# TensorE's fillers before the second loop over slots cut from 26 to 3, and two of four tile sums moved from TensorE to VectorE and GpSimd

## What is computed

```python
x = x + 0.5 * ffn(layernorm(x))
x = x + attn(layernorm(x))          # gated linear attention in chunks of 64
x = x + 0.5 * ffn(layernorm(x))

def ffn(x):                          # 16 experts of width 176, 4 for each token
    shared = silu_and_mul(x @ shared_gate_up_w.T) @ shared_down_w.T
    shared = shared * sigmoid(x @ sgate_w.T)
    topk_w, topk_ids = top_k(softmax(x @ gate_w.T), 4)
    ...
        coef = sum(where(topk_ids == e, topk_w, 0))
        acc = acc + (silu_and_mul(x @ w13_e.T) @ w2_e.T) * coef
    return shared + acc
```

## Time and profile before

| | us |
|---|---|
| median of 3 runs | 464.55 (464.35 to 465.01) |
| the profiled execution, its own time | 462.54 |
| its span, first to last instruction | 460.7 |
| TensorE busy | 422.1 (92% of the span) |
| VectorE busy | 279.0 (61%) |
| ScalarE busy | 215.2 (47%) |
| GpSimd busy | 197.3 (43%) |

### The profile page before, as it was taken

How to read it: one execution, slowest core, us unless ns; L and a number is a source line. 1 busy time by engine, 2 the same in 40 slices (tenths; PEclk the granted TensorE clock), 3 DMA queues, 4 the chain that set the end, 5 groups by cost and what they waited for, 6 DMA issues and landing times.

```text
span 460.7 us, 9122 instructions
## 1 busy us (share of the span) xinstructions
PE 422.1 (92%) x2288; PEld 327.5 (71%) x2293; DVE 279.0 (61%) x871; ACT 215.2 (47%) x575; POOL 197.3 (43%) x213
## 2 busy tenths in 40 slices
PE   6698985999999999996997988999999999999997
PEld 3455552888887999562477975655679999999855
DVE  5646968566565666297287546634256666666554
ACT  2265636455555666251755642211036666656510
POOL 6177840144444444490044413777114444444530
PEclk9599998899999999997998989999999999999999
DMA  7999942456667442740000008994314444444174
GB/s 253 379 407 233 357 161 58 159 194 218 248 247 293 145 138 79 296 200 0 0 0 1 2 1 338 421 364 153 102 50 128 143 133 138 140 131 134 71 298 168
DMA packets 37376, 80.41 MB, mean 175 GB/s; under 512 B 5680, under 2 KB 27056, under 8 KB 35824
## 3 DMA queue, kind: packets, MB, share of 16 engines
q1 hardware_dynamic: 29744, 58.07, 37.4%
q0 software_dynamic: 7584, 21.77, 12.7%
HBM read 44.28 MB, written 35.54 MB: 173 GB/s over the span
## 4 chain that ended last, share of the span: by engine, by line
PE 77%; DVE 11%; issue 3%; POOL 3%; ACT 3%; DMA 2%; DVEq 0%; SPq 0%
PE ps L466 7%; PE ps L517 7%; PE ps L521 7%; PE ps L518 7%; PE ps L488 6%; PE ps L500 6%; PE ps L471 5%; PE ps L529 4%; PE ps L642 4%; PE ps L547 3%; POOL WR L1029 3%; PE ps L549 2%; PE ps L548 2%; PE ps L553 2%; PE ps L551 2%
## 5 line engine op out<-in xcount | busy, mean ns | idle before, releaser
L986 POOL DMA_INDIRECT results<-ar,idx x94 | 90.4, 962 | 146.7 <-ACT ar L815 143.5
L978 POOL DMA_INDIRECT slots<-XR,pos x64 | 65.3, 1021 | 45.6 <-DVE pos L1159 27.0
L1199 DVE SCALAR_TENSOR_TENSOR ar<-ps,XR,ar 128x176 f32<-128x176 f32 x94 | 37.7, 401 | 66.8 <-ACT ar L801 66.8
L517 PE MATMUL ps<-WH,xt 128*128 x188 | 63.1, 336 | 5.7 <-issue 4.1
L518 PE MATMUL ps<-WL,xt 128*128 x188 | 61.2, 326 | 0.0
L801 ACT ACTIVATE ar<-ps 128x176 f32<-128x176 f32 x94 | 29.9, 318 | 64.9 <-PE ps L521 64.1
L488 PE MATMUL ps<-WS,ar 128*128 128x256 f32 (+1 forms) x192 | 45.7, 382 | 4.0 <-DVE ar L1079 2.3
L488 PEld LDWEIGHTS ps<-WS,ar 128*128 128x128 f32 (+1 forms) x192 | 35.8, 189 | 18.2 <-issue 7.9
L521 PE MATMUL ps<-WH,xl 128*128 x188 | 46.8, 331 | 1.2 <-DVE xl L1216 1.2
L1216 DVE TENSOR_TENSOR xl<-ps,xt 128x256 fp32r<-128x256 f32 x94 | 39.9, 424 | 12.3 <-ACT xt L796 5.6
L466 PE MATMUL ps<-XT,WS 128*128 128x512 f32 x96 | 47.2, 616 | 0.0
(11 more groups left out here) (164 smaller groups left out, 844.1 us busy)
## 6 DMA issues: line engine op xcount, KB each, us to landing
XR<-slots SPq DMA_DIRECT2D x94, 144.0 KB, 2.2
WR<-results SPq DMA_DIRECT2D x16, 512.0 KB, 6.9
WR<-w SPq DMA_DIRECT2D x4, 1408.0 KB, 15.6
wl<-WL SPq DMA_DIRECT2D x4, 1408.0 KB, 5.6
WL<-wl SPq DMA_DIRECT2D x4, 1408.0 KB, 10.1
slots<-zeros SPq DMA_DIRECT2D x33, 144.0 KB
W2R<-w2a SPq DMA_DIRECT2D x1, 2048.0 KB, 23.8
w2l<-W2L SPq DMA_DIRECT2D x1, 2048.0 KB, 7.1
```

Of the source, the lines that this page charges most:

```text
L517: pe.matmul(to, token, WH[:, bass.ds(e, 1), k, :].rearrange("p a n -> p (a n)"), start=k == 0, stop=False)
L978: pool.indirect_dma_start(out=slots_dram[:, :], out_offset=bass.IndirectOffsetOnAxis(ap=pos[:, t, r:r + 1], axis=0), in_=XR[:, t, :], in_o ...
L986: pool.indirect_dma_start(out=results_dram[:, :], out_offset=bass.IndirectOffsetOnAxis(ap=idx[:, i:i + 1], axis=0), in_=ys[i % NY], in_off ...
```

## The change

There are three edits. The 18 fillers in front of the second loop's first transposes are gone, and the 8 behind them are 3. The border between the two ways of summing is moved from `NT // 2` = 4 to `SUMMED` = 6: tiles 4 and 5 of the second feed-forward stage go the way of tiles 0 to 3. The semaphore counts in `added_to` and `combine` follow.

```diff
+        SUMMED = NT - 2
+
         def by_tensor(f, t):
-            return f == 1 and t >= NT // 2
+            return f == 1 and t >= SUMMED
...
-            return 2 * NT + 3 * min(t + 1, NT // 2) + max(t + 1 - NT // 2, 0)
+            return 2 * NT + 3 * min(t + 1, SUMMED) + max(t + 1 - SUMMED, 0)
...
-                keep_warm((6, 18)[f], 6)
+                if f == 0:
+                    keep_warm(6, 6)
                 pe.wait_ge(s_tab, f + 1)
                 e = [None] * TL
                 e[0] = expert(0)
                 slot_turn(f, 0)
-                keep_warm(8, 6)
+                keep_warm((8, 3)[f], 6)
...
                 if by_tensor(f, t):
-                    dve.wait_ge(s_cmb, t - NT // 2 + 1)
+                    dve.wait_ge(s_cmb, t - SUMMED + 1)
```

## The result

The changed kernel takes 460.05 us in the median of 4 runs (459.46 to 461.74), against 464.78 (464.35 to 466.69, also 4 runs) for the kernel before on the same chip. The ratio is 0.9896 with a 95% interval from 0.9857 to 0.9936: faster, by 4.7 us or 1.0%.

A forecast was written before the change was run, and what follows sets the result against it. TensorE holds 77% of the chain that ended last, with fillers as links at the second loop's entry. Terms -4.1 (entry) and -0.5 (tail) sum to -4.6 us: median 464.55 to about 460.0, range 458.6 to 462.1.

The forecast's parts named there:

- The 18 in front: Second loop's entry: without these fillers the first transposes start 3.66 us earlier, nothing else holding them.
- The 8 behind, now 3: Behind the first transposes: three fillers hide under ScalarE's copy of `xt`; worth 0.8 us taken by itself.
- What is late next: Entry: `xl`, behind VectorE's four additions, stalls L521 until about 332.65; gain 4.1 us, 0.4 of 4.5 lost.
- Behind L521 the loop is as before: Rest of the second loop after its first L521: claimed unchanged, so the entry's 4.1 us is kept.
- The tail: Tile sums at the end: two tiles moved from TensorE to VectorE and GpSimd gain 0.5 us, bounds 1.45 and -0.45.
- The meetings: Tail: VectorE additions running beside GpSimd's cost 0.47 us more each; two more meetings cost 0.94 us.
- 2.0 us per tile for 4 and 5: Tail: VectorE's time per moved tile, three additions 1.37, then 0.12, 0.48 and 0.04 us.
- A: Rival: tail meetings cost nothing, or `xl` does not stall; -5.55 or -5.95 us, 458.6 to 459.0. Chance 0.12.
- B: Rival: the tail gives nothing or loses 0.45 us, meetings at their dearest; -3.65 us, 460.9. Chance 0.13.
- C: Rival: the clock falls at the second loop's entry, costing 2.4 us; -2.2 us, 462.4. Chance 0.12.
- D: Rival: the clock falls and stays down, slower than before; 20 us of it gives +2.4, 467.0. Chance 0.03.
- E: Rival: something else holds the first transposes until near 334, so fillers' time is hidden; say 464.1. Chance 0.02.

The follow-up runs named there:

- e3: Kernel before with 36 fillers instead of 18 in front of the second loop's transposes; entry 13.82 us, ratio 1.0069.
- e6: Changed kernel with no fillers at the second loop's entry; entry 5.70 us, first tiles 10.72 us.
- e5: Changed kernel with 8 fillers instead of 3 behind the second loop's first transposes; entry 6.04 us.
- e4: Changed kernel with VectorE computing the first `xl` ahead of its four shared-part additions; entry 5.21 us, first tiles 10.64 us.
- e7: Changed kernel with the second loop's first transposes waiting for VectorE's four additions, TensorE idle 1.80 us; entry 7.20 us.
- e12: Changed kernel with the sums' border at tile 5 and the first `xl` ahead of the four additions; entry 5.21 us, tail 20.94 us.
- after: The changed kernel itself, against the kernel before; 460.05 us median, ratio 0.9896.
- e8: Changed kernel with no tile sums by TensorE, all eight tiles by VectorE and GpSimd; tail 24.66 us, ratio 0.992.
- e1: Changed kernel with the fillers' part alone, sums' border back at tile 4; entry 5.70 us, tail 22.81 us, ratio 0.9895.
- e2: Changed kernel with the sums' part alone, fillers back at 18 and 8; entry 9.93 us, tail 21.77 us, ratio 1.0011.
- e10: Changed kernel with the sums' border at tile 5 instead of 6; tail 21.16 us, ratio 0.9886.

## Why the prediction was right

**The total.** Forecast 460.0 us, -4.6; measured 460.05 and -4.73 in the median. That the two agree to 0.05 us is chance: the interval of the ratio is 3.7 us wide, and the errors of the terms, -0.1 at the entry, +0.3 in the first tiles and -0.34 at the end, cancel in part.

**The 18 in front: right.** Nothing else held the transposes. The dose of e3 gives 0.217 us per filler, for 0.213 forecast. The transposes came 3.46 us behind the start of the last 16 records and not 7.33, so the step was worth 3.87, for 3.66: the forecast has them start where the fillers had started, and they start 0.2 earlier.

**The 8 behind, now 3: right.** The three are hidden (e6), and eight cost 0.34 more (e5), not the 1.07 of a count.

**What is late next: right, its time 0.1 us too long.** L523 came 5.70 behind the last 16 records. The forecast put it at 332.65 - 326.82 = 5.83. Undoing VectorE's order (e4) takes away the stall and 0.49 us.

**"Behind L521 the loop is as before": wrong by 0.3 us in the first tiles.** They took 10.75 against 10.45. The prediction had the register read's bare price as 0.3 us, at the first transposes, where it was hidden. One tile later the transposes came 0.25 us late behind the stalled L523: 0.11 in the stalled product, and 0.14 where the read stands. The four kernels with the fillers in front cut in which L523 does not stall (e4, e5, e7, e12) take 10.50 to 10.64, and the seven in which it does 10.72 to 10.85. That the stall costs this is shown by these; that the 0.14 are the read's is read from its start in the trace, and was not tried by itself. In the loop as a whole, 0.3 us can't be told: on the chips without the 35 us it takes 98.87 to 99.36 where nothing stalls and 99.13 to 99.71 where L523 does.

**The tail: right in mechanism, its gain undersized, 0.84 us against 0.5.** The meetings cost as forecast: six plus three additions took 5.10 us, where the six before took 2.73 and three more make 4.10; 1.0 us for 0.94. The two of "about 0.9 us" are there, 0.947 and 0.946. The step that was mis-sized is "2.0 us per tile for 4 and 5" and 1.02 with 0.04 between for 6 and 7. The rows after give 1.92 (451.38 to 453.30) and 0.92 (453.30 to 454.22). With VectorE never waiting, the next addition starts 0.40 us after the start of a shared part of 0.48. The tail's rows of before, where VectorE waited for TensorE each time, don't show this overlap, but the four shared parts at the entry do: they take 1.66 us for four of 0.48 or a little less. From the end of tile 4's third addition (446.17 + 5.10 = 451.27) to the end at 455.61 it took 4.34, for 4.74 by the forecast's terms. That is 0.4 us less, and with the 0.06 more for the meetings it is the 0.34 by which the gain was undersized.

The rule of the Trainium skill (SBUF — State Buffer, on who interferes with whom) fits in kind: additions as long as 0.947 us beside GpSimd's, none over 0.427 without them. In size it fits roughly. What was left of GpSimd's addition when VectorE's began was 0.67 us both times (446.61 to 447.28, 448.01 to 448.67), and VectorE's took 0.52 more than alone.

**The rivals.** A is out: the meetings are there (0.947 us), and so is the stall on `xl` (e4). Its 1.45 at the tail is not reached. B's loss at the tail is out. C and D, the clock, did not occur: 1.00 in all stretches from the entry to 354 us in after, e6 and e7. That is shown only for this place and these idle times, one execution each. E is out: the transposes came at once, and e3 shows the fillers bare.

**Why the profiled spans differ by 2.9 us and the medians by 4.7.** Entry, loop and tail together fell from 131.8 to 126.6, or 5.15 us. The part ahead took 2.2 more in this one execution. The clock was granted less in these three stretches of it, with the same program, and in others a little more (0.97 against 0.94 from 180 to 236 us). How much of the 2.2 us it accounts for was not separated. Changed kernel:

```profile
72.00:86.00 14.00, 8.64 (x29) 6.81 (x28) 8.92 (x21) 5.88 (x11) 0.00 (x0) 0.65 0.08 23
...
236.00:256.00 20.00, 15.92 (x99) 13.94 (x99) 15.03 (x36) 9.65 (x30) 11.50 (x17) 0.83 0.00 1
268.00:282.00 14.00, 12.71 (x54) 9.03 (x55) 7.62 (x32) 4.63 (x21) 1.09 (x2) 0.76 0.32 112
```

Kernel before:

```profile
72.00:86.00 14.00, 8.00 (x34) 6.15 (x33) 9.29 (x21) 6.41 (x12) 0.00 (x0) 0.76 0.08 23
...
236.00:256.00 20.00, 15.92 (x104) 13.92 (x104) 16.11 (x39) 10.57 (x34) 12.57 (x17) 0.91 0.00 1
268.00:282.00 14.00, 12.71 (x62) 9.24 (x61) 7.62 (x32) 4.61 (x21) 0.61 (x1) 0.88 0.28 97
```

## What to carry to other kernels

Before fillers are priced by their count, ask what they cover: find the engine that comes ready last once they are gone (here VectorE behind four additions that nobody there waited for), and look what stands in the stalled instruction's queue behind it, such as a register read. When work moves from the matrix engine to the vector engine at the end of a program, price a tile on either side, count the meetings with GpSimd as time of the vector engine, and put the border where both are done together. For changes of 1 us in 460, compare stretches between two fixed instructions, and set their borders close to the change. The entry and the end repeat to 0.01 us in most traces here and the tail only within 0.7, while whole runs of one kernel differ by several us.

## What was not expected of the hardware

**The clock from run to run.** The same instructions ahead of the second loop started the loop's entry between 325.8 and 331.4 us into the span in the runs on the faster chips (e8 and e7). The granted clock differs in the stretches shown above; how much of the spread is due to it was not separated.

**On one chip ScalarE stood still for 33 to 36 us.** On the chip of e1, ScalarE waited once for 35.88 us ahead of a shared unit of the second stage, where the kernel before on the first chip has it wait 5.91 at most:

```profile
336.15 1.09 ACT L793 ACTIVATE ar<-ps 128x512 f32<-128x512 f32 x2 [35.88 <-remote]
```

In the same time SyncE's instructions for the zeroing of slots took up to 0.71 us each, register moves included, where they take 0.03 on the first chip:

```profile
L375 SPq MOVE slots<-zeros x16: 17/29/709, 310.0 to 343.7; - x16
```

GpSimd went on at its pace. The other traces from that chip have it too, with 35.92 us (e4), 32.56 (e2) and 32.57 (e10). The unchanged kernel is slower there by the same amount, so it is no matter of the change; its cause was not tried and stays open.
